# A recommendation model's forward pass: other places for field products, layers 2 to 4 and scratch writes around the interaction half-stages

## The reference

```
h = relu(dense @ dw1 + db1); dense_emb = relu(h @ dw2 + db2)
emb = concatenate([dense_emb[:, None, :], emb_tables[f_ids, sparse_idx]], axis=1)
pairs = einsum('bfd,bgd->bfg', emb, emb)[:, iu0, iu1]        # i < j
z = relu(concatenate([emb.reshape(B, -1), pairs], axis=1) @ ow1 + ob1)
z = relu(z @ ow2 + ob2); z = relu(z @ ow3 + ob3); return z @ ow4 + ob4
```

## Time and profile before

| | us |
|---|---|
| median of 3 runs | 188.66 |
| the three runs | 187.3, 188.84, 188.66 |
| profiled execution, device time | 187.21 |
| its span in the profile | 185.4 |
| TensorE busy in the span | 127.4 |
| GpSimd busy in the span | 123.8 |

### The profile page before, as it was taken

One profiled execution on the slowest core, in us unless ns is written; L12 is line 12 of the kernel. 1 busy time (PEld: TensorE's weight loads), 2 busy tenths in 40 slices (PEclk: granted clock), 3 DMA queues, 4 the chain that ended last, 5 costly groups with the idle time before them and its releaser, 6 DMA issues.

```text
span 185.4 us, 3069 instructions
## 1 busy us (share of the span) xinstructions
PE 127.4 (69%) x1301; PEld 68.8 (37%) x1301; DVE 37.8 (20%) x97; ACT 42.2 (23%) x96; POOL 123.8 (67%) x199
## 2 busy tenths in 40 slices
PE   1510285828655995839439993959729979989994
PEld 0000132514344442524226432424426446656453
DVE  2700003000142204100144005000234023136011
ACT  0440310031046201040075001040174011166011
POOL 3888888888735888888565888888367887200000
PEclk9999999975965699996965798587997999999999
DMA  5999532221212332312312332222222324100000
GB/s 157 409 332 357 172 26 23 23 28 21 21 13 23 21 22 24 28 22 26 24 13 24 23 27 20 23 28 20 19 20 20 22 25 31 18 4 0 4 0 0
DMA packets 4576, 9.80 MB, mean 53 GB/s; under 512 B 2065, under 2 KB 2065, under 8 KB 3922
## 3 DMA queue, kind: packets, MB, share of 16 engines
q0 software_dynamic: 3328, 3.41, 21.3%
q1 hardware_dynamic: 1010, 5.30, 7.1%
q10 hardware_dynamic: 224, 0.89, 1.6%
HBM read 9.59 MB, written 0.00 MB: 52 GB/s over the span
## 4 chain that ended last, share of the span: by engine, by line
PE 45%; POOL 26%; issue 18%; ACT 5%; DMA 3%; DVE 2%
PE acc L259 20%; POOL gathered L211 20%; PE acc L292 10%; PE inter L276 7%; POOL pace L219 6%; PE acc L310 4%; DMA gathered<-tables,rows 2%; ACT emb L386 1%; ACT emb L387 1%; PE turned L240 1%; PE acc L301 1%; ACT pairs L392 1%; DMA idx_raw<-idx 1%; ACT z L399 1%; DVE emb L466 1%
## 5 line engine op out<-in xcount | busy, mean ns | idle before, releaser
L211 POOL DMA_INDIRECT gathered<-tables,rows x104 | 98.9, 951 | 34.6 <-issue 16.9
L259 PE MATMUL acc<-w,emb 128*128 128x512 f32 x104 | 65.7, 780 | 19.4 <-issue 12.3
L259 PEld LDWEIGHTS acc<-w,emb 128*128 128x128 f32 x104 | 31.3, 315 | 46.3 <-issue 36.9
L392 ACT ACTIVATE pairs<-inter 28x96 f32<-28x96 f32 (+1 forms) x64 | 15.7, 246 | 39.8 <-PE inter L276 39.1
L219 POOL MEMSET pace<- 128x192 uint8 x90 | 24.7, 274 | 0.1
L292 PE MATMUL acc<-w,pairs 128*128 128x512 f32 x56 | 24.7, 592 | 0.0
L182 DVE COPY pairs<-inter 28x96 f32<-28x96 f32 (+1 forms) x64 | 17.0, 266 | 26.5 <-PE inter L276 25.8
L276 PE MATMUL inter<-emb 64*28 64x28 f32 x1024 | 12.6, 204 | 13.8 <-DMA gathered<-tables,rows 10.1
L240 PE MATMUL turned<-small,gathered 128*128 128x128 f32 x52 | 10.1, 317 | 13.5 <-DMA gathered<-tables,rows 13.5
L386 ACT ACTIVATE emb<-turned 128x512 f32<-128x512 f32 x8 | 8.8, 1098 | 45.7 <-issue 28.6
L465 DVE COPY emb<-turned 128x512 f32<-128x512 f32 (+1 forms) x7 | 5.5, 784 | 64.1 <-issue 49.5
(11 more groups left out here) (47 smaller groups left out, 26.3 us busy)
## 6 DMA issues: line engine op xcount, KB each, us to landing
w<-w SPq DMA_DIRECT2D x5, 1024.0 KB, 8.7
gathered<-tables,rows POOLq DMA_INDIRECT x104, 3.4
small<-small_pack ACTq DMA_DIRECT2D x1, 706.5 KB, 6.0
dense_sb<-dense_pack ACTq DMA_DIRECT2D x1, 160.5 KB
idx_raw<-idx SPq DMA_DIRECT2D x1, 39.0 KB
idx_raw<-idx SPq DMA_DIRECT2D x1, 13.0 KB, 1.9
out<-y SPq DMA_DIRECT2D x1, 2.0 KB
```

Source lines behind the costliest of these rows:

```text
L211: pool.indirect_dma_start(out=gathered[:, t, s, :], out_offset=None, in_=tables, in_offset=bass.IndirectOffsetOnAxis(ap=rows[:, t, s:s + 1 ...
L259: nc.tensor.matmul(acc[t][:], emb[:, tile_of(t), place(2 * c)], w[:, c, :], start=(c == 0), stop=False)
L392: last = move(lambda dst, src: nc.scalar.activation(dst, src, ACT.Copy), t, k, (0, 1))
```

## The change

- TensorE's order in tiles 0 to 2: `turn(t, 2)` and `turn(t, 3)` follow each other, then come the products of two chunks of group 2 (chunks 8 and 9) and the first half-stage. The products of chunks 10, 11 and 12 stand behind `turn(t+1, 0)`, ahead of the second half-stage.
- Layers 2 to 4 run in three parts (`PARTS`). 256 samples go beside tile 2, between the products of its group 1, with layer 3 in the bank `acc[3]`; 128 samples (those of tile 2) beside tile 3, layer 2 ahead of the products of group 1, layer 3 between the last two half-stages, layer 4 behind the last field products; 128 samples at the end, as before, behind a wait for the first two outputs.
- Tile 3 has five groups (`LAST_GROUPS`): 4, 4, 2, 2 and 1 chunks. In each, transposes, copies and products follow that split.
- `UNPACED_FROM` is gone: each gather that isn't held has a scratch write.

The core of the difference:

```
+LAST_GROUPS = [(0, 4), (4, 8), (8, 10), (10, 12), (12, 13)]
-EARLY = LAST * P
+PARTS = [slice(0, 2 * P), slice(2 * P, 3 * P), slice(3 * P, B)]
-UNPACED_FROM = 18
...
                         if held:
                             pool.wait_ge(inter_done, 2 * (t - 1) + HOLDS.index(s) + 1)
-                        elif t < LAST or s < UNPACED_FROM:
+                        else:
                             nc.gpsimd.memset(pace[:, t * NF + s, :], 0)
...
                 turn(t, 0)
                 if t:
+                    field_products(t - 1, 2, 2)
+                    field_products(t - 1, 3)
                     interactions(t - 1, 1)
                 field_products(t, 0)
...
                 turn(t, 1)
-                if t < LAST:
+                if t == LAST:
+                    break
+                if t == LAST - 1:
+                    layer2(PARTS[0], 1, whole, (acc[0], acc[1]))
+                    field_products(t, 1, 0, 2)
+                    layer3(PARTS[0], 0, acc[3])
+                    field_products(t, 1, 2)
+                    layer4(PARTS[0], 0, acc[0])
+                else:
                     field_products(t, 1)
-                    turn(t, 2)
-                    field_products(t, 2)
-                    turn(t, 3)
-                    field_products(t, 3)
-
-            layer2(early, LAST - 1, [[(m, k) for m in range(2) for k in range(K1)]], (acc[0], acc[1]))
...
+                turn(t, 2)
+                turn(t, 3)
+                field_products(t, 2, 0, 2)
+
+            layer2(PARTS[1], 2, whole, (acc[1], acc[2]))
+            field_products(LAST, 1)
             turn(LAST, 2)
             turn(LAST, 3)
+            field_products(LAST, 2)
+            turn(LAST, 4)
             interactions(LAST, 0)
+            layer3(PARTS[1], 1, acc[1])
+            field_products(LAST, 3)
             interactions(LAST, 1)
-            field_products(LAST, 3)
+            field_products(LAST, 4)
+            layer4(PARTS[1], 1, acc[2])
             pair_product(LAST)
```

More of the change, by code:

```diff
@@ L61, with groups @@
 ALU = mybir.AluOpType
+def groups(t):
+    return LAST_GROUPS if t == LAST else GROUPS
 def place(field):
@@ L124, in build @@
         ones_set = sem("ones_set")
-        group_in = [[sem(f"group_in{t}_{g}") for g in range(NG)] for t in range(TILES)]
+        group_in = [[sem(f"group_in{t}_{g}") for g in range(len(groups(t)))] for t in range(TILES)]
         gathers_held = sem("gathers_held")
@@ L207, in _ @@
                     pool.wait_ge(rows_done, 1)
-                for g, (c0, c1) in enumerate(GROUPS):
+                for g, (c0, c1) in enumerate(groups(t)):
                     for s in range(2 * c0, 2 * c1):
@@ L231, in turn @@
             def turn(t, g):
-                c0, c1 = GROUPS[g]
+                c0, c1 = groups(t)[g]
                 pe.wait_ge(group_in[t][g], 2 * (c1 - c0) * 16)
@@ L241, in turn @@
                                              gathered[:, t, 2 * c:2 * c + 2, :].rearrange("p f d -> p (f d)"), ident)
[L242 removed]
+                if t == LAST and g == NG:
                     moved(t - 1)
@@ L248, in kept, with field_products @@
             def kept(t, g):
[L250 to L254, removed]
+                if g % 2 or g == NG:
+                    pe.wait_ge(kept_dve, t * 2 + g // 2 + 1)
+                if g % 2 == 0:
+                    pe.wait_ge(kept_act, t * 2 + g // 2 + 1)
+            def field_products(t, g, first=0, end=W_GROUP):
                 if t == 0:
@@ L257, in field_products @@
                 kept(t, g)
-                for c in range(*(chunks or GROUPS[g])):
+                c0, c1 = groups(t)[g]
+                for c in range(c0 + first, min(c0 + end, c1)):
                     nc.tensor.matmul(acc[t][:], emb[:, tile_of(t), place(2 * c)], w[:, c, :],
@@ L266, in interactions @@
                         pe.wait_ge(dense_placed, 1)
-                    kept(t, 2)
-                    kept(t, 3)
+                    for g in range(2, len(groups(t))):
+                        kept(t, g)
                     if t:
@@ L326, in layer4 @@
                 nc.tensor.matmul(bank[0:1, 0:n], ow4, z3t[:, samples], start=True, stop=True).then_inc(y_mm, 1)
-            early, late = slice(0, EARLY), slice(EARLY, B)
             at_once = [(0, K1)]
+            whole = [[(m, k) for m in range(2) for k in range(K1)]]
             for t in range(TILES):
@@ L499, in _ @@
                 keep(t, 1)
+                if t == LAST - 1:
+                    z2_relu(PARTS[0], 0, acc[1])
+                    outputs(PARTS[0], 0, acc[0])
                 if t == LAST:
[L501 to L506 removed]
+                    z2_relu(PARTS[1], 1, acc[2])
+                keep(t, 3)
+            dve.wait_ge(group_turned, LAST * NG + NG + 1)
+            nc.vector.tensor_copy(evens(LAST, NG), turned_all(LAST, NG)).then_inc(kept_dve, 1)
             moves(LAST, 0)
             moves(LAST, 1)
+            outputs(PARTS[1], 1, acc[2])
             z1_features(LAST, Z1_STEPS)
[L510 to L511 removed]
+            z2_relu(PARTS[2], 2, acc[2])
+            outputs(PARTS[2], 2, inter[0])
 def lay_out(inputs):
```

67 lines of the change are left out of this document (26 added, 41 removed).

## The result

The changed kernel takes 191.67 us (median of 4 runs, 189.99 to 193.01), against 188.5 for the kernel before (4 runs with the three above). The ratio is 1.015, with a 95% interval from 1.008 to 1.023: slower, by about 3 us. Every ratio here leaves out runs over 1.5% above the fastest of their kernel (193.01 is one), so it can differ from the quotient of the medians. The forecast was 190.3, +0.9%. The profiled execution took 191.83 us with a span of 190.0, which is 4.6 more than the 185.4 of before.

What follows compares the result with a forecast made beforehand. The prediction took the order of the chain as the bound: paced gathers, held until TensorE finishes half-stages. Terms -2.1 + 1.0 + 2.6 + 0.15 = +1.65 us on 188.66 gave 190.3 us, range 185.6 to 193.3.

Steps and rivals of the forecast that it cites:

- Term 3: Tiles 0 to 2: three chunks between the halves delay second half-stages and all later gathers, +2.6 us.
- term 1: Layers 2 to 4 moved into tile 2, plus five groups, end TensorE's lateness in tile 3: -2.1 us.
- signs of being right: No idle before second half-stages, 8.4 to 8.9 us after gather 7; POOL wait over 3; low clock; last gather 160.5 to 163.
- signs of being wrong: PE idle before second half-stages, PE busy when last group lands, a hole inside one, or tile 2's first half-stage late.
- rival C: Tail does not regain its 2.1 us, leaving second half-stages alone, +2.6 and no more from pacing: 191.4 us, chance 0.05.
- nothing long: Tile 3: after gather 25 lands, only one chunk's two transposes, their copies and the interactions follow.
- Term 2: Scratch writes behind the last eight gathers: seven steps of 1.39 instead of 1.25 us delay the last gather, +1.0 us.
- 3.4 us after gather 7: Tiles 0 to 2: the next tile's transposes start once gather 7 has landed, 3.4 us after its start.
- Term 4: Second half-stages, now without 3 us of idling ahead: a hole could cost 0 to 1.1 us each, taken as 0.
- rival B: Clock returns late or second half-stages get the hole: slower, 193.1 to 194.1 us, chance 0.2.
- Term 5: End stage: layer 3 of 128 samples between halves, one chunk instead of three behind; +0.15 us for small joints.
- Rival A: Three chunks between the halves fit into the gathers' time at 2.4 GHz: faster, 184.9 us, chance 0.2.

Runs made afterwards that it cites:

- the chunks alone: Kernel before with only the chunk order changed in tiles 0 to 2 (two chunks ahead of the first half-stage, three between); 189.98 us against 187.26, ratio 1.013.
- five ahead: Changed kernel with the products of all five chunks ahead of the first half-stage again, in the order of before; 185.73 us against 187.26, ratio 0.994.
- four ahead: Changed kernel with four chunks ahead of the first half-stage and one between the halves; 182.95 us against 184.5, ratio 0.993.
- three ahead: Changed kernel with three chunks ahead of the first half-stage and two between the halves; 188.64 us, ratio 1.021 to the kernel before.
- parts alone: Changed kernel with the chunk order of before and no late scratch writes, leaving the three layer parts and five groups; 188.26 us, ratio 1.002.
- kept warm: Changed kernel with idle time ahead of the first half-stage filled by field products whose result is unused; 188.25 us against 184.5, ratio 1.017.

## Why the prediction was right

The direction and the place were right, and the median lies inside the range (185.6 to 193.3), 1.4 above the point. The mechanism, that POOL waits for second half-stages which their own chunks hold back at the low clock, was shown by its parts: the chunks alone lose 1.3%, all five ahead or four ahead lose nothing, and the clock kept up in tile 0 takes the distance from 8.8 to 9.5 down to 7.2. The size was not right: +1.65 us was forecast, the medians show +3.2 and the traces +4.6. Term 3 was 1.8 us too low and term 1 counted on 1.4 us that did not come; both err the same way. That the number is inside all the same owes much to the width of the range, 7.7 us, and so is in part luck.

Of the signs of being right one came in full: no idle ahead of the second half-stages. The distances were 8.62, 11.11 and 9.22 instead of 8.4 to 8.9. POOL's wait behind gather 10 was over 3 us in one tile only (2.17, 3.31, 2.97). The clock was 0.50 when the products between the halves started, but 1.00 at the second half-stages. The last gather came at 163.62, not by 163, and the interactions 5.85 behind it, not 4.5. Of the signs of being wrong one came, that of rival C: TensorE was still busy when the last group landed (about 167.0, 3.4 us behind 163.62; its transposes start at 168.04). C's time of 191.4 is the nearest of all, but C gave the tail nothing back and put no pacing in. The terms:

- Term 1 (-2.1): it was -0.7. The lateness did go, but my step that "nothing long" stands behind it missed two things. ScalarE copied the transposes of chunks 8 and 9 late, 1.71 us after they had ended. And TensorE, finished early, idles 2.24 us, the clock falls, and the two chunks take 3.27 instead of the 1.7 of the fast rate. With five or four ahead that wait was 0.2 to 0.3 us, the clock stayed up, and the interactions came 5.05 and 4.76 behind the last gather, some 1.5 to 1.8 better than before: near the term. The wait's price is not fixed: with 2.25 to 2.27 us of it in five traces of the second chip the interactions came 4.7 to 5.2 behind the last gather, and some of the low clock fell behind them (three ahead: 5.3 us from half to half instead of 3.7); in parts alone 2.12 us of idle at this place left the clock at 1.00. The added layers beside tile 2 cost nothing, as said.
- Term 2 (+1.0): the last gather moved by 0.94, 1.18 and 1.27 us in the three pairs. What it does to the time is not settled, not even its sign: without the writes the ratio is 0.1% higher (changed kernel), 0.8% higher (five ahead) and 0.4% lower (four ahead), and in the kernel before they change 0.1%. The late copies on "remote" stand in kernels with and without the writes.
- Term 3 (+2.6): it was +4.4, the step that was mis-sized. From the transposes to the second half-stage I took 5.2 us; it was 4.67, 5.83 and 5.47, in the mean 5.3. The error is in "3.4 us after gather 7": the transposes started 3.95, 5.28 and 3.75 after it, since the first half-stages ended later than the data landed. I let the holes of the first half-stages vanish with the longer idling; they didn't, and tile 1 got a second one of 1.29 us, a late block of instructions, which the prediction's sum has nowhere. That adds 2.8 us to the three distances. Against it stand 1.3 us that I had put at nothing: three second half-stages at 2.4 GHz last 1.27 each, not 1.65 to 1.74.
- Term 4 (0): right: no second half-stage of tiles 0 to 2 had a hole in any kernel. But the holes' true place was the first half-stages, and rival B did not name them.
- Term 5 (+0.15): -0.1.

Rival A would have needed the full clock. In kept warm only tile 0 had it for the whole stretch, and even there the distance was 7.2 and not 6.8, as the transposes started 3.88 us after gather 7. By the Trainium skill ("Runtime: NRT & Kernel Launch", Instruction fetch mechanics) crossing a block is mostly hidden. Here, in seven traces, at least one fetch of the ten or eleven is not: its hole is 1.3 to 2.8 us long. The measurement decides. Why this block is fetched ahead in some orders of the program (at 75 to 80 us) and in others only 0.6 to 1.0 us before the hole or within it stays open; moving the block's end by 48 or 240 places did not make it be fetched ahead, filling the idle time or a fourth chunk ahead did.

## What to carry to other kernels

Work that fills an engine's idle time is free only if it fits in the clock that the engine has at that moment: price it at the low clock when a wait stands ahead of it, above all where another queue is held until it is done. Where a queue waits on a burst of many small instructions, look in the timeline for holes with the releaser "issue" and in the DMA view for instruction blocks in that stretch; a reorder that changes nothing in the burst can still put such a fetch inside it. And a stage that gets done early may idle long enough to run its last piece slower.

## What the runs showed that was not expected

- A missing block of instructions stops TensorE for 1.3 to 2.8 us, at a fixed place of the program (behind 120 passes; behind 118 with 4 instructions more ahead, 97 with 48, 128 with 240), and TensorE goes on 1.35 to 1.45 us after the block's transfer has ended.
- The half-stage's 128 thin passes of 28 columns take 1.27 us at 2.4 GHz and 1.71 at 1.2 GHz, so even these follow the clock, if not in proportion.
- The same kernel before differs by 1.5% between two chips (187.26 and 184.5 us). The changed kernel ran in two comparisons, with 191.67 and 192.1 us, in which the kernel before had 188.5 and 184.2, so the ratio of the two was 1.015 in one and 1.035 in the other.
